# Counting stage of a graph kernel: when VectorE reads its group bounds, and where ScalarE adds the bias to the projection

## What is computed

```python
q = einsum('nd,hdk->nhk', x, Wq) + bq          # k, v and the skip term alike
scores = sum(q[dst] * k[src], axis=-1) / 8     # layer 0: attention over the edges
alpha = segment_softmax(scores, dst)
agg = segment_sum(alpha * v[src], dst)
...                                            # layer 1: attention with leaky_relu terms
agg = segment_sum(relu(x[src]), dst)           # layer 2: plain sums over the edges
...                                            # layer 3: a normalised sum and an attention
```

## Time and profile before

| | |
|---|---|
| median of 3 runs | 3530.02 us (3528.23 to 3532.93) |
| the profiled execution | 3525.65 us, its span 3524.0 us |
| granted TensorE clock over the span | 0.979 of full speed |
| busy share of the span | PE 94%, PEld 76%, DVE 74%, ACT 59%, POOL 19% |
| counting stage | from 0 to about 563 us, 16% of the span |
| in 300 to 400 us (counting) | PE 93.9 us, DVE 85.2, ACT 56.0, POOL 9.9; granted clock 0.92; DMA 0.55 busy, 213 GB/s |

### The profile page before, as it was taken

The page is one execution under the profiler, slowest core; times in us unless marked ns, Lnnn a source line. Parts: engine busy times, 40 slices in busy tenths (PEclk is TensorE's granted clock), DMA queues, the critical chain, the costliest instruction groups (busy, mean ns, idle before and its releaser), DMA issues. The chain is left out here.

```text
span 3524.0 us, 67249 instructions
## 1 busy us (share of the span) xinstructions
PE 3324.4 (94%) x25814; PEld 2694.6 (76%) x25815; DVE 2623.1 (74%) x4799; ACT 2078.5 (59%) x3840; POOL 652.2 (19%) x604
## 2 busy tenths in 40 slices
PE   5999997999999999997999999999899999999998
PEld 3555555888888888885777777777688888878887
DVE  8888885777767777766999999999599443236665
ACT  2555555777767767775999999999211111115454
POOL 1001000011111111111245236666100100000000
PEclk9999998999999999998999999999999999999999
DMA  2545558233333333426333533333666565553341
GB/s 83 222 193 218 217 212 262 94 113 124 107 106 130 106 106 106 131 85 203 107 114 112 193 109 106 132 106 113 219 222 222 194 213 191 205 211 140 133 149 58
DMA packets 202700, 534.72 MB, mean 152 GB/s; under 512 B 56881, under 2 KB 165462, under 8 KB 168502
## 3 DMA queue, kind: packets, MB, share of 16 engines
q1 hardware_dynamic: 199494, 526.25, 43.2%
q10 hardware_dynamic: 1904, 3.81, 0.4%
q0 software_dynamic: 1024, 0.82, 0.1%
HBM read 362.87 MB, written 167.80 MB: 151 GB/s over the span
## 5 line engine op out<-in xcount | busy, mean ns | idle before, releaser
L1141 PE MATMUL a_p_t<-ident,a_sm 128*128 128x128 f32 x5000 | 901.6, 279 | 33.3 <-ACT a_sm L1215 19.5
L1215 ACT ACTIVATE a_sm<-a_p_t 128x896 f32<-128x896 f32 (+3 forms) x800 | 668.4, 836 | 331.5 <-PE a_p_t L1141 286.3
L1209 ACT ACTIVATE a_sm<-a_sm,a_negm 128x896 f32<-128x896 f32 (+3 forms) x600 | 702.3, 1170 | 49.3 <-DVE a_negm L1272 49.0
L1141 PEld LDWEIGHTS a_p_t<-ident,a_sm 128*128 128x128 f32 x5000 | 616.5, 142 | 144.6 <-issue 113.4
L1168 PE MATMUL a_p_o<-a_sm,a_v 128*64 128x128 f32 x10000 | 701.8, 279 | 16.5 <-ACT a_sumT L1222 16.3
L1300 DVE CUSTOM_DVE_ANT_0 a_sm<-a_p_s,sh_rows 128x400 f32<-128x400 f32 x790 | 439.9, 571 | 288.8 <-PE a_p_s L1123 253.2
L1168 PEld LDWEIGHTS a_p_o<-a_sm,a_v 128*64 128x64 f32 x10000 | 557.2, 137 | 122.0 <-issue 73.1
L1123 PE MATMUL a_p_s<-sh_kt,sh_q 128*128 128x400 f32 x1580 | 588.2, 432 | 34.4 <-DVE a_mx L1300 19.9
L1123 PEld LDWEIGHTS a_p_s<-sh_kt,sh_q 128*128 128x128 f32 x1580 | 305.4, 194 | 58.4 <-DVE a_mx L1300 29.4
L1321 DVE SCALAR_TENSOR_TENSOR a_sm<-sh_wide,sh_al 128x3125 f32<-128x3125 f32 x100 | 346.8, 3468 | 4.1 <-PEq L54 2.4
L1331 DVE CUSTOM_DVE_ANT_0 a_sm<-a_sm,sh_rows 128x3125 f32<-128x3125 f32 x100 | 348.5, 3485 | 1.0
(11 more groups left out here) (319 smaller groups left out, 4873.4 us busy)
## 6 DMA issues: line engine op xcount, KB each, us to landing
sh_rows<-d_full SPq DMA_DIRECT2D x67, 1600.0 KB, 7.0
sh_ct<-d_ct SPq DMA_DIRECT2D x50, 1600.0 KB, 6.6
d_ct<-sh_wide SPq DMA_DIRECT2D x25, 1600.0 KB, 5.3
d_full<-sh_rows SPq DMA_DIRECT2D x25, 1600.0 KB, 5.8
t_third<-d_ct SPq DMA_DIRECT2D x25, 1600.0 KB, 6.7
d_logs<-sh_rows SPq DMA_DIRECT2D x23, 1664.0 KB, 6.0
sh_rows<-d_logs SPq DMA_DIRECT2D x23, 1664.0 KB
sh_q<-d_q SPq DMA_DIRECT2D x200, 64.0 KB, 2.3
```

Source lines behind the costliest of these rows:

```text
L1141: m = nc.tensor.transpose(p_t[u % 2][:, i * P:(i + 1) * P], sm[buf][:, a * P:(a + 1) * P], ident[:, :])
L1209: nc.scalar.activation(sm[buf][:, c], sm[buf][:, c], ACT.Exp, bias=negm[:, buf:buf + 1], accum_out=parts[:, buf, e:e + 1]).then_inc(s_prob, 1)
L1215: nc.scalar.activation(sm[buf][:, a_row[u] * P:a_row[u + 1] * P], p_t[u % 2][:, 0:turns[u] * P], ACT.Copy).then_inc(s_copy, 1)
```

## The change

VectorE no longer reads a tile's 12 words with one `TENSOR_LOAD`. A helper `words` reads 2 words and 4 words ahead of each half, so four loads a tile. The operations of the projection (`proj.dve`, `dve_out`) keep their place between the two tiles' one-hot rows, but in the program they now stand behind the loads of the next tile's first half, ahead of its rows, where before they stood ahead of the load. ScalarE does `act_high` behind the second logarithm, no longer ahead of the first (in tile 0, which has no logarithms, it stays).

```diff
@@ -580,15 +580,22 @@
+                def words(j, o, n):
+                    _, said = nc.values_load_multi_w_load_instructions(
+                        meta[0:1, bass.ds(j, 1), o:o + n].rearrange("p n k -> p (n k)"), engines=[dve.engine], min_val=0, max_val=(1 << 16) - 1, skip_runtime_bounds_check_because="loaded as unsigned 16-bit words")
+                    return said
+
                 def tile(j, par, half, first=False, last=False):
-                    _, said = nc.values_load_multi_w_load_instructions(
-                        meta[0:1, bass.ds(j, 1), :].rearrange("p n k -> p (n k)"), engines=[dve.engine], min_val=0, max_val=(1 << 16) - 1, skip_runtime_bounds_check_because="loaded as unsigned 16-bit words")
                     for k in range(QPT):
-                        rows_of(j * QPT + k, k, said[2 * k], said[2 * k + 1], said[2 * QPT + k * QUAD:2 * QPT + (k + 1) * QUAD])
-                    if not first:
-                        proj.dve(dve, j - 1)
-                    proj.dve_out(dve, j)
+                        trips_of, first_of = words(j, 2 * k, 2), words(j, 2 * QPT + k * QUAD, QUAD)
+                        if k == 0 and not first:
+                            if not (isinstance(j, int) and j == 1):
+                                proj.dve(dve, j - 2)
+                            proj.dve_out(dve, j - 1)
+                        rows_of(j * QPT + k, k, trips_of[0], trips_of[1], first_of)
                 tile_loop(dve, tile)
+                proj.dve(dve, NT - 2)
+                proj.dve_out(dve, NT - 1)
                 proj.dve(dve, NT - 1)
@@ -742,9 +749,12 @@
                 def tile(j, par, half, first=False, last=False):
                     collect(j, par, half, 0)
-                    proj.act_high(act, j)
+                    if first:
+                        proj.act_high(act, j)
                     for t in range(4 if not first else 0):
                         log(*before(j, par, half), t)
+                        if t == 1:
+                            proj.act_high(act, j)
                     collect(j, par, half, 1)
```

## The result

| | before | changed |
|---|---|---|
| median (range, runs) | 3529.12 us (3523.37 to 3532.93, 4) | 3558.03 us (3546.69 to 3559.32, 4) |
| ratio, 95% interval | | 1.0075 (1.0056 to 1.0094) |
| profiled execution, its span | 3525.65, 3524.0 us | 3546.69, 3544.7 us |
| granted clock over the span | 0.979 | 0.987 |
| one tile, 21 tiles from L237 to L237 | 20.31 us | 21.77 us |

The change makes the kernel 0.75% slower, 29 us by the medians. The forecast was 3498 us (3488 to 3518) with a chance of 0.07 for slower: it was wrong, in sign too.

A forecast was written before the change was run, and what follows sets the result against it. PE and ACT were taken to set the pace, DVE trailing through one wait; with DVE then bounding at 18.7 us, 21 tiles save 33.8 us, less 1.2, rounded to 32: median 3498 us, range 3488 to 3518.

The forecast's parts named there:

- ScalarE's part: Logarithms ahead of `act_high` on ScalarE: half 1 of the count 0.97 us earlier, PE's tile 18.05 us at full clock.
- VectorE becomes the bound: Counting stage: DVE's tile of 18.7 us exceeds PE's 18.05, so PE waits some 0.7 us a tile for `hot_k`.
- The pair between the tiles: DVE's loads of 2 and 4 words between tiles: 1.65 us, leaving a bubble of 0.55 us ahead of L236.
- Getting ahead of the wait: On DVE's sequencer the load no longer stands behind the wait for `act_high`, where it stood some 2 us.
- the second rival: DVE's load is held until queued operations drain, so nothing moves: 3524 to 3532 us; no difference overall had chance 0.06.
- The clock rival: PE's clock still falls in every tile, PE's tile of 19.65 us bounds, 3517 us; chance 0.15.
- VectorE, the load that is moved: DVE's step pricing the moved loads: two bubbles add 1.30 us to 17.40, a tile of 18.7 us.
- the pair between the halves: DVE's loads of 2 and 4 words between halves, where no load was: 1.5 us, a bubble of 0.75 us.
- first tiles: DVE in tiles 0 to 2: new bubbles where little was idle, in sum 1.2 us later.
- everything behind the stage is untouched: The kernel after the counting stage: no change in time, so the stage's 32 us gain carries to the total.
- The slower-side rival: Four DVE loads cost by the instruction, 2.84 us a pair, a tile of 21.2 us: 3550 us; chance 0.07.
- break-even: DVE's loads: at 2.4 us a pair the tile would stay at 20.31 us, with no gain or loss.

The follow-up runs named there:

- act_only: The kernel before with ScalarE's part alone, VectorE keeping its one load of 12 words: 3498.26 us, ratio 0.9891.
- four_ahead: The changed kernel with all four loads between the tiles and none between the halves: 3516.82 us in one run.
- experiment 6: Stores cut by columns: counts and logarithms in 4 in the changed kernel, 3533.6 us; logarithms in 8 with one load ahead and old ScalarE order, 3528.6 us.
- dve_only: The changed kernel with ScalarE's part taken back, so VectorE's part alone: 3564.18 us, ratio 1.0082.
- eight_four: Kernel before with ScalarE's part; VectorE loads 8 words between L237 and `dve_out`, 4 behind `dve_out`: 3489.33 us, ratio 0.9871.
- one_mid: Kernel before with ScalarE's part and VectorE's one load of 12 words moved between L237 and `dve_out`: 3489.08 us, ratio 0.9874.

## Why the prediction was wrong

**Sound.** *ScalarE's part:* PE's wait for L741 was to fall below 0.3 us a tile; none is left. The clock was to stay up once that idle was gone; it is 1.00 in the window of 100 to 500 us. As a single edit this part gives 3498.26 us. That this is my predicted time is chance: the forecast reached it with VectorE's tile at 18.7, and `act_only` has 19.01 with the old load.

*VectorE becomes the bound:* yes; PE waits for `hot_k`, DVE never for `act_high`. *The pair between the tiles:* 0.52 + 0.95 = 1.46 us against 1.65, gaps of 0.38 and 0.79 against 0.55. *Getting ahead of the wait:* yes; the load ran at 203.8, beside queued operations, so the second rival ("VectorE does not get ahead of the wait") falls. *The clock rival* falls.

**The step that failed** is "VectorE, the load that is moved", in its price for the pair between the halves: 1.5 us taken, 1.85 at most, 1.73 + 2.97 = 4.70 us measured. The bubble was 3.91 us in place of 0.75; 17.40 + 3.78 + 0.58 = 21.8 replaces 18.7. The rest of the tile's sum was right to 0.2 us.

How the price went wrong is worth more than its size. I divided 3332 ns by 12 words and called 278 ns the rate "beside the transfers". That treats the 3.33 us as one condition. Windows of the kernel before over that load (232.2 to 235.5) show three, the end of the log store, the small stores of v and skip, and quiet:

```profile
232.20:233.20 1.00, 0.94 (x4) 1.00 1.00 426
233.20:234.20 1.00, 0.00 (x0) 0.51 0.74 253
234.20:235.50 1.30, 0.00 (x0) 0.50 0.02 7
```

At the quiet rate of 2708/12 = 226 ns the last 1.3 us are 5.8 words, so 6.2 words took the first 2.0 us: some 320 ns each as an estimate, 1.4 times the quiet rate and not 1.2 times. That gives 1.9 us for a pair, a tile of 19.1 us, and 24 us of gain in place of 32. So the larger part of the miss does not come from the division. The new loads took 1.73/2 = 0.87 and 2.97/4 = 0.74 us a word, more than twice what the old place shows beside its traffic, and no row of before holds that price. The old load (232.2) started over 4 us behind the issue of the log store (227.92) and met its end; the new ones have the counts, q and k and then the whole start of the log store beside them.

What was missing is the question what runs where the new loads go. The step "where there was no load" was costed on the scale of the old place, although SP's queue in the trace of before shows stores of counts, keys and logarithms in every tile. The *first tiles* (1.2 us forecast, 5.9 measured) have the same fault. A second term was put at nothing: "everything behind the stage is untouched". In the profiled executions that part took 16 us less in the changed kernel (open point b), so a stage that ends 36.8 us later makes the whole 21 us longer there.

**The slower-side rival** had the right sign (chance 0.07, 3550 us against 3558 measured) and the wrong mechanism: it priced by the instruction, which `four_ahead` refutes. Its break-even was useful all the same, as it named how dear a pair may be, 2.4 us; the new place had 4.70. It took the stretch of traffic as 1.44, out of the same mean over a long load.

By the Trainium skill, page "DMA: Bandwidth & Descriptors", section "Latency and other measured facts", a `tensor_load` has a floor of about 600 ns. The trace disagrees for 2 words in quiet: 501 to 518 ns in the changed kernel and `four_ahead`. That floor would have moved the sum by 5 us and had no part in the miss.

**What stays open.** (a) What in the stores slows the load; see experiment 6. (b) The stage ends 36.8 us later in the profiled execution, while the whole is 21 us longer there and 29 us by the medians. What lies behind the stage (span less the last L431) took 2964 us before and 2948 in the changed kernel. Windows over that part, before and changed, show the same work at the same clock:

```profile
559.80:3524.00 2964.20, 2835.99 (x23126) 2398.86 (x23126) 2157.23 (x3993) 1792.92 (x3330) 593.16 (x560) 0.99 0.43 143
```

```profile
596.60:3544.70 2948.10, 2833.05 (x23126) 2397.27 (x23126) 2155.36 (x3993) 1791.79 (x3328) 594.45 (x560) 0.99 0.43 144
```

PE is busy 3 us less in the changed kernel and idle 13 us less. In the other ten kernels, whose later stages are the same program, this part took 2954 us in `dve_only`, whose stage ends as late as in the changed kernel (597 us), and 2960 to 2972 in the nine whose stage ends by 567 us. So it was short where the stage ended late. It is one execution of each, and the kernel before itself ranged over 3517.84 to 3546.74 us in later runs; no run tells whether the one follows from the other. (c) `eight_four` was to be faster than `one_mid` and is not. The dearer second load (0.16 to 0.39 us over quiet) accounts for a part of the distance between 18.3 and 18.65 us; the rest was not tested.

## What to carry to other kernels

Price an instruction at the place it moves to, not where it stood: list what every queue has in flight there, and look whether that phase is locked by dependences (then it is there every time) or drifts. When a row lies only partly beside traffic, cut it by windows before you divide by its words; a mean over both parts hides the price that a shorter instruction will pay in full. And test the parts of an edit apart: here one part alone gained 1.1% (`act_only`), and adding the other took it to 0.75% slower.

## What the runs showed of the hardware that was not expected

VectorE's load of registers from the table in SBUF takes about 0.22 us a word in quiet (4 words 0.95, 12 words 2.71; 2 words 0.51), and cutting 12 words into four instructions costs only 0.2 us more. Beside this kernel's own DMA stores it stretches far more than a data operation does: 2 words 1.73 us, 4 words up to 3.26 us, 12 words 4.17 us where a log store of 1664 KB runs beside about the first half of them. In the same stretch VectorE's `hot_k` took 1.39 us beside the stores and 1.40 without. Cutting the log store's rows to an eighth changed nothing (4.12 us). So a wait for such a load can be a wait for other engines' traffic, though the list of waits calls it "issue" and names nobody.
